# Cross-attention's query as three rounded products, in a decoder block on one core

## What is computed

```python
def _layernorm(x, axis=-1, eps=1e-05):
    ...
    return (x - m) / jnp.sqrt(v + eps)

def _L0_xattn_ref(k, v, q, Wk, Wv, bv, Wq, bq, Wo, bo):
    kp = jnp.einsum('bsd,ed->bse', k, Wk)
    vp = jnp.einsum('bsd,ed->bse', v, Wv) + bv
    qp = jnp.einsum('bsd,ed->bse', q, Wq) + bq
    scale = 1.0 / jnp.sqrt(jnp.float32(kp.shape[-1]))
    scores = jnp.einsum('bqd,bkd->bqk', qp, kp) * scale
    probs = jax.nn.softmax(scores, axis=-1)
    ctx = jnp.einsum('bqk,bkd->bqd', probs, vp)
    return jnp.einsum('bqd,ed->bqe', ctx, Wo) + bo
...
x = x + _L0_attn_ref(_layernorm(x, axis=-1), ...)
x = x + _L0_xattn_ref(ctx_1024, ctx_1024, _layernorm(x, axis=-1), ...)
x = x + _L0_ffn_ref(_layernorm(x, axis=-1), ...)
```

## Time and profile before

| | |
|---|---|
| median of 3 runs | 2769.6 us |
| profiled execution, its own time | 2767.93 us |
| span of the profiled execution | 2766.1 us |
| mean granted TensorE clock | 0.972 |
| TensorE matmul busy | 2549.4 us (92%), 19090 records |
| VectorE busy | 1976.6 us (71%), 3087 |
| ScalarE busy | 1442.4 us (52%), 4247 |
| GpSimd busy | 862.9 us (31%), 811 |
| query of cross-attention on TensorE | 1024 records, 201.3 us |
| `xnxT` copies on ScalarE | 64, 31.0 us |

### The profile page before, as it was taken

One profiled execution on the slowest core, in us unless ns is written; L12 is line 12 of the kernel. 1 busy time (PEld: TensorE's weight loads), 2 busy tenths in 40 slices (PEclk: granted clock), 3 DMA queues, 4 the chain that ended last, 5 costly groups with the idle time before them and its releaser, 6 DMA issues.

```text
span 2766.1 us, 55689 instructions
## 1 busy us (share of the span) xinstructions
PE 2549.4 (92%) x19090; PEld 2107.2 (76%) x19090; DVE 1976.6 (71%) x3087; ACT 1442.4 (52%) x4247; POOL 862.9 (31%) x811
## 2 busy tenths in 40 slices
PE   5999999999999999999999999999999999999840
PEld 3678878887888788878887888788878887888620
DVE  4445778877777787777777787777777877776552
ACT  2445555555555555555555555555555555555343
POOL 0001333323333333233333332333333323233344
PEclk9999999999999999999999999999999999999965
DMA  6233455554444555444445454444454554443799
GB/s 188 57 79 80 108 133 128 134 129 137 123 121 115 132 126 136 129 134 123 124 115 132 124 137 129 132 128 121 117 132 123 137 129 131 127 122 105 198 213 201
DMA packets 131545, 358.88 MB, mean 130 GB/s; under 512 B 21908, under 2 KB 26516, under 8 KB 123269
## 3 DMA queue, kind: packets, MB, share of 16 engines
q0 software_dynamic: 63520, 160.60, 25.0%
q1 hardware_dynamic: 63190, 192.16, 24.7%
q10 hardware_dynamic: 4784, 5.46, 0.6%
HBM read 316.38 MB, written 41.78 MB: 129 GB/s over the span
## 4 chain that ended last, share of the span: by engine, by line
PE 78%; DVE 8%; ACT 5%; issue 4%; DMA 2%; POOL 1%; ACTq 1%; DVEq 0%; POOLq 0%
PE psX L1150 41%; PE psA L1150 17%; PE psA L1159 6%; PE psF L1150 5%; PE psA L1216 4%; PE psA L1239 3%; PE psX L1159 2%; ACT L769 1%; DMA vg<-in_L_ffn_aux_values,idx 1%; DVE xmax L955 1%; PE psF L1159 1%; DVE top L1006 1%; ACT xT_hi L687 1%; DVE oT_lo L902 1%; DVE idx L1009 1%
## 5 line engine op out<-in xcount | busy, mean ns | idle before, releaser
L613 POOL DMA_INDIRECT vg<-in_L_ffn_aux_values,idx x512 | 542.8, 1060 | 1208.1 <-issue 1071.3
L708 ACT ACTIVATE pa<-psA,nmax 112x224 f32<-112x224 f32 x1024 | 443.6, 449 | 191.3 <-DVE nmax L924 184.5
L924 DVE TENSOR_REDUCE nmax<-psA 112x4 f32<-112x896 f32 x256 | 267.2, 1086 | 151.8 <-PE psA L1216 151.8
L1035 DVE SCALAR_TENSOR_TENSOR agg<-vg,wt,agg 112x512 f32<-112x512 f32 x406 | 361.6, 891 | 10.7
L1150 PE MATMUL psX<-big,gT 128*112 128x375 f32 x1024 | 333.4, 478 | 0.6 <-ACT gT L735 0.6
L1150 PE MATMUL psX<-pT,cx 125*128 125x224 f32 x1536 | 299.1, 355 | 0.0
L1150 PEld LDWEIGHTS psX<-pT,cx 125*128 125x128 f32 x1536 | 288.0, 190 | 4.0 <-issue 0.3
L939 DVE TENSOR_TENSOR pa<-pa,rsum 112x896 f32<-112x896 f32 x256 | 279.6, 1092 | 8.8
L1150 PEld LDWEIGHTS psX<-big,gT 128*112 128x112 f32 x1024 | 175.5, 176 | 125.7 <-issue 0.9
L1159 PE MATMUL psA<-ident,pa 112*112 112x112 f32 x2048 | 229.4, 263 | 24.9 <-DVE oT_lo L902 24.9
L1159 PEld LDWEIGHTS psA<-ident,pa 112*112 112x112 f32 x2048 | 202.0, 134 | 57.2 <-DVE oT_lo L902 31.5
(11 more groups left out here) (211 smaller groups left out, 5915.7 us busy)
## 6 DMA issues: line engine op xcount, KB each, us to landing
big<-in_ctx_t SPq DMA_DIRECT2D x32, 1500.0 KB, 6.3
cx<-in_ctx SPq DMA_DIRECT2D x32, 1344.0 KB
xa<-in_x SPq DMA_DIRECT2D x64, 224.0 KB, 2.9
centered<-in_x_t SPq DMA_DIRECT2D x32, 448.0 KB, 4.6
x<-in_L_attn_bff POOLq DMA_DIRECT2D x32, 448.0 KB
x<-cb_scratch POOLq DMA_DIRECT2D x32, 448.0 KB, 5.7
x<-in_x SPq DMA_DIRECT2D x31, 448.0 KB, 5.1
out<-x SPq DMA_DIRECT2D x30, 448.0 KB, 3.3
```

What stands on the lines that cost most here:

```text
L613: pool.indirect_dma_start(vg[:, c % SLOTS, k, :], None, aux_values, bass.IndirectOffsetOnAxis(ap=idx[:, t, n:n + 1], axis=0))\
L708: last = nc.scalar.activation(pa[:, t, h, :], psA[0:R, h, t * S:(t + 1) * S], ACT.Exp, bias=nmax[:, k % 2, h, t:t + 1], accum_out=rsum[:, ...
L924: nc.vector.tensor_reduce(nmax[:, k % 2, h:h + 2, :], psA[0:R, h:h + 2, 0:T * S].rearrange("p h (t s) -> p h t s", t=T), AX_X, ALU.max, ne ...
L1035: last = nc.vector.scalar_tensor_tensor(dst, vg[:, c % SLOTS, k, :], w, dst, ALU.mult, ALU.add)
```

## The change

The query becomes a `product3`. At set-up ScalarE rounds each chunk of the folded weight (with the scale) to `m1_hi` and VectorE makes `m1_lo` from the bank; before, VectorE alone wrote the chunk. In each batch ScalarE's two copies of the turned rows become rounding casts into `xnxT_hi`, which no longer free the bank but count `xn_hi`; VectorE gets a step in `("X", "turn")`, `x_turn_lo`: two subtractions that read the bank and `xnxT_hi`, write `xnxT_lo`, and free the bank. `xnxT_lo` lies over `oT_hi`, and `m1_hi` over the old `m1`. No table of order is changed. Cut to its core:

```diff
@@ -162,7 +162,9 @@
         wff_at = (nc.sbuf_base + 31) // 32 * 32
         wffT = (sb("wff_hi", [P, C, D], F32R), sb("wff_lo", [P, C, D], F32R))
         over_wff = nc.alloc_sbuf_tensor_at("over_wff", [P, 2 * C, D], F32, offset=wff_at)
+        m1_at = (nc.sbuf_base + 31) // 32 * 32
         m1 = sb("m1", [P, C * D])
+        m1T = (nc.alloc_sbuf_tensor_at("m1_hi", [P, C, D], F32R, offset=m1_at), sb("m1_lo", [P, C, D], F32R))
         m2_at = (nc.sbuf_base + 31) // 32 * 32
         m2 = (sb("m2_hi", [P, C, D], F32R), sb("m2_lo", [P, C, D], F32R))
         over_m2 = nc.alloc_sbuf_tensor_at("over_m2", [P, 2 * C, D], F32, offset=m2_at)
@@ -190,6 +192,7 @@
         rsum = sb("rsum", [R, NB, T, HB])
         pa = sb("pa", [R, T, HB, S])
         paT = sb("paT", [R, T, HB, S])
+        oT_at = (nc.sbuf_base + 31) // 32 * 32
         oT = (sb("oT_hi", [P, C, S], F32R), nc.alloc_sbuf_tensor_at("oT_lo", [P, C, S], F32R, offset=centered_at))
         big = sb("big", [P, C * SK])
         cxT = big[:, :].rearrange("p (c k) -> p c k", c=C)
@@ -200,7 +203,8 @@
         xnf = xnx
         px = nx[:, :].rearrange("p (t k) -> p t k", t=T)
         xnxT_at = (nc.sbuf_base + 31) // 32 * 32
-        xnxT = sb("xnxT", [P, C, S])
+        xnxT = (sb("xnxT_hi", [P, C, S], F32R), nc.alloc_sbuf_tensor_at("xnxT_lo", [P, C, S], F32R, offset=oT_at))
+        over_xnxT = nc.alloc_sbuf_tensor_at("over_xnxT", [P, C, S], F32, offset=xnxT_at)
         gT_at = (nc.sbuf_base + 31) // 32 * 32
         gT = sb("gT", [P, C, S])
         uT = (nc.alloc_sbuf_tensor_at("uT_hi", [P, C, S], F32R, offset=xnxT_at),
@@ -273,6 +277,7 @@
         summed, agg_stored = sem("summed"), sem("agg_stored")
         xT_hi, qk_hi, rq_hi, uT_hi, oT_hi = (sem(f"{n}_hi") for n in ("xT", "qk", "rq", "uT", "oT"))
         m2_hi, wff_hi, wff_split = sem("m2_hi"), sem("wff_hi"), sem("wff_split")
+        m1_hi, xn_hi = sem("m1_hi"), sem("xn_hi")
         small_loaded, mask_loaded = sem("small_loaded"), sem("mask_loaded")
         steps = {s: sem(f"dve_step_{s}") for s in "NAXFG"}
         log_done, lsum_spread, mean_full = sem("log_done"), sem("lsum_spread"), sem("mean_full")
@@ -384,8 +389,7 @@
         qw = cx[:, C * D:(C + 1) * D]
         rwT = gT[:, 0, 0:RS]
         over_d = gT[:, 1, 0:P]
-        bv_rows = xnxT[:, :, 0:R]
-        m1v = weight(m1)
+        bv_rows = over_xnxT[:, :, 0:R]
 
 
         CENTERED = 3
@@ -680,6 +684,12 @@
                         copy_out(s, job, b, dst[:, 2 * j:2 * j + 2, :], chunks(s, job))
                 return step
 
+            def x_turn_hi(b, _):
+                for j in range(2):
+                    job = FILL["X", "turn", 0] + j
+                    wait_full(act, "X", job, b)
+                    nc.scalar.copy(xnxT[0][:, 2 * j:2 * j + 2, :], chunks("X", job)).then_inc(xn_hi, 1)
+
             def center_hi(b, _):
 
                 act.wait_ge(xt_scaled, b + 1)
@@ -799,6 +809,10 @@
                 act.wait_ge(setup_full, ROUTED + c + 1)
                 nc.scalar.copy(m2[0][:, c, :], spare(ROUTED + c)).then_inc(m2_hi, 1)
 
+            def m1_hi_half(_, c):
+                act.wait_ge(setup_full, BIASED + c + 1)
+                nc.scalar.activation(m1T[0][:, c, :], spare(BIASED + c), ACT.Copy, scale=float(D) ** -0.5).then_inc(m1_hi, 1)
+
             def log_var(*_):
                 act.wait_ge(var_taken, B)
                 nc.scalar.activation(var_all[:, :], var_all[:, :], ACT.Ln, bias=1.0, accum_out=lsum[:, :])\
@@ -825,9 +839,9 @@
                 last.then_inc(scaled, 1)
 
             pipeline(act, {("Z", "log"): log_var, ("Z", "gate"): logits, ("Z", "scale"): scale,
-                           ("W", "split"): split_hi, ("W", "wff"): wff_hi_half, ("W", "m2"): m2_hi_half, ("N", "center"): center_hi, ("A", "mix"): mixed,
+                           ("W", "split"): split_hi, ("W", "wff"): wff_hi_half, ("W", "m2"): m2_hi_half, ("W", "m1"): m1_hi_half, ("N", "center"): center_hi, ("A", "mix"): mixed,
                            ("A", "qk"): qk, ("Q", "qk"): qk, ("A", "value"): value, ("A", "score"): exp_scores, ("A", "prob"): probs_turned,
-                           ("X", "turn"): turn("X", "turn", xnxT), ("X", "query"): query,
+                           ("X", "turn"): x_turn_hi, ("X", "query"): query,
                            ("X", "score"): x_exp, ("X", "prob"): x_probs_turned, ("X", "mix"): x_mixed,
                            ("F", "turn"): turn("F", "turn", xnfT), ("F", "route"): route, ("F", "score"): f_score,
                            ("F", "top"): f_top})
@@ -948,6 +962,13 @@
                 wait_full(dve, "X", j, b)
                 nc.vector.tensor_tensor(x1[:, t, :], bank("X", j)[0:R, :], x1[:, t, :], ALU.add)\
                     .then_inc(drained["X"][j % banks["X"]], 1)
+
+            def x_turn_lo(b, _):
+                for j in range(2):
+                    job = FILL["X", "turn", 0] + j
+                    dve.wait_ge(xn_hi, 2 * b + j + 1)
+                    lo(xnxT[1][:, 2 * j:2 * j + 2, :], bank("X", job)[:, 0:2 * S].rearrange("p (c s) -> p c s", c=2),
+                       xnxT[0][:, 2 * j:2 * j + 2, :]).then_inc(drained["X"][job % banks["X"]], 1)
 
             def x_maxima(b, t):
                 for j in range(2):
@@ -1089,7 +1110,9 @@
                 nc.vector.tensor_tensor(cb[:, :], made_next()[0:R, :], cb[:, :], ALU.add).then_inc(setup_drained, 1)
 
             def made_m1(_, c):
-                nc.vector.tensor_scalar(m1v[:, c, :], made_next(), float(D) ** -0.5, None, ALU.mult).then_inc(setup_drained, 1)
+                dve.wait_ge(m1_hi, c + 1)
+                nc.vector.scalar_tensor_tensor(m1T[1][:, c, :], made_next(), float(D) ** -0.5, m1T[0][:, c, :].bitcast(F32),
+                                               ALU.mult, ALU.subtract).then_inc(setup_drained, 1)
 
             def made_gb(*_):
                 nc.vector.tensor_scalar(gb[:, :], made_next()[:, 0:C], float(D) ** -0.5, None, ALU.mult)\
@@ -1136,7 +1159,7 @@
                            ("N", "stat"): x_moments, ("X", "stat"): x_stat, ("F", "stat"): f_stat, ("N", "center"): center_lo, ("A", "qk"): qk, ("Q", "qk"): qk,
                            ("A", "score"): maxima, ("A", "share"): share, ("A", "mix"): o_lo,
                            ("X", "enter"): x_enter,
-                           ("X", "norm"): x_norm, ("X", "score"): x_maxima, ("X", "prob"): x_probs_turned,
+                           ("X", "norm"): x_norm, ("X", "turn"): x_turn_lo, ("X", "score"): x_maxima, ("X", "prob"): x_probs_turned,
                            ("X", "mix"): u_lo, ("X", "out"): x_out,
                            ("F", "norm"): f_norm, ("F", "route"): route, ("F", "learn"): learn, ("F", "top"): f_top,
                            ("G", "sum"): g_sum, ("F", "sum"): g_sum})
@@ -1258,8 +1281,8 @@
                     wait_free(pe, "X", job, b)
                     for k in range(2):
                         i = 2 * j + k
-                        last = product(bank("X", job)[:, k * S:(k + 1) * S],
-                                       [(m1v[:, c, i * P:(i + 1) * P], xnxT[:, c, :]) for c in range(C)])
+                        last = product3(bank("X", job)[:, k * S:(k + 1) * S],
+                                        [(both(m1T, ALL, c, slice(i * P, (i + 1) * P)), both(xnxT, ALL, c, ALL)) for c in range(C)])
                     filled("X", job, last)
 
             def x_scores(b, t):
```

## The result

| | before | after |
|---|---|---|
| median of the runs | 2769.8 us (2767.4 to 2774.8, 11 runs) | 2775.7 us (2772.0 to 2780.7, 11 runs) |
| profiled execution | 2767.93 us | 2772.72 us |
| one iteration, mean of 28 | 79.11 us | 79.35 us |

The ratio is 1.0023, with a 95% interval of 1.0014 to 1.0032: slower, by little more than the 0.2% that can be told from nothing.

What follows compares the result with a forecast made beforehand. TensorE was taken to set the time nearly everywhere. 29 iterations x 0.31 = 9.0, two x -0.62 = -1.2 and set-up 1.0 gave +8.8 us: median 2778.4, rounded down to 2778; range 2750 to 2789, likeliest case 2775 to 2784.

Steps and rivals of the forecast that it cites:

- TensorE, the query: Query of each batch: 48 rounded matmuls at 0.111 us take 5.33 us for 6.16, 0.83 less; ends 0.62 earlier.
- VectorE, the new wait: Two subtractions between nx and stats_F: stats_F starts 2.73 us later, 1.57 of it waiting for transposes and copies.
- Nmax at 1418.19: Maxima of the scores, behind the sums: lag 2.73 exceeds the 2.07 of cover, so start moves 0.66 from 1417.53.
- X score 1 starts 0.31 later: Second half of the cross scores: waits 0.9 us for its bank, starts 0.31 us later; whole iteration 0.31 longer.
- The early iterations: Second and third iterations, lacking sums or router: the lag is covered there, -0.62 us each.
- Set-up: Before the loop: four ScalarE casts ahead of the drains of the folded weight, +1.0 us, bounds 0 and 2.5.
- "nothing" for the last batch: Last batch, after the loop: waits some 0.8 us for the subtractions and saves 0.83, so nothing.
- The cover holds: Rival, sums ahead of nmax: shifted from GpSimd's addition, VectorE regains up to 1.97 us; 2751 us; chance 0.24.
- The 2727 that the prediction worked out from four passes: Query by the skill's four passes for true fp32: gain 32 x (1.54 - 0.21) = 43 us, 2727.
- It cancels: Rival: release edges 0.15 shorter or lag 0.2 smaller; -0.2 to +0.16 us per iteration, 2764 to 2775; chance 0.23.
- The wait grows: Rival: no overlap of subtractions, held second cast or late gathers; iteration 0.5 to 0.9 longer, 2784 to 2796; chance 0.11.
- The clock: Rival: new waits drop TensorE to 1.2 GHz for a stretch; in every iteration 80 us, 2850; chance 0.02.

Runs made afterwards that it cites:

- Experiment 3: The kernel of experiment 2, with VectorE still waiting in X turn until ScalarE has made both casts, without subtracting: 2763.45 us, ratio 0.9974.
- experiment 2: The change without its two subtractions, all three products taking the rounded rows (the rest of the rows left out): 2748.67 us, ratio 0.9921.
- experiment 4: The complete change with the two subtractions moved behind both passes of the router's statistics and ahead of their merging: 2753.52 us, ratio 0.9939.
- experiment 6: TensorE starts the query after the first subtraction: added to the kernel of experiment 4, 2747.02 us; added to the change as it is, 2774.28 us.

## Why the prediction was right

**TensorE, the query: right, the gain a little large.** 48 matmuls between 1413.36 and some 0.11 behind 1418.70 are 5.45 us with the first step of 0.21; the forecast was 5.33 and 0.06 for the first load. The query begins 0.05 behind the second subtraction, which ends at 1413.31, and not 0.14. In the chain of the change it ended 0.55 earlier than before, where 0.62 was forecast. Without a wait the chain has 5.37, so that the form alone saves 0.70 and not the 0.83 of the pace. The long first step is not the wait's doing: rounded matmuls begin so without one too, as in the kernel before:

```profile
1464.89 0.37 PE L1150 MATMUL psA<-xT_hi,wqT_hi 128*128 128x224 f32 x1
1465.10 0.28 PE L1150 MATMUL psA<-xT_lo,wqT_hi 128*128 128x224 f32 x1
```

That a short pass has a fixed part fits the trace of before: passes of 256 columns step every 0.115 us (27 steps from 1402.47 to 1405.58), those of 224 columns every 0.111, some 4% less for 12.5% fewer columns. The shapes of the weights differ as well (112 and 128 columns), so the size of that part is not shown.

**VectorE, the new wait: right to 0.01.** Idle 1.56 for 1.57. Stats_F starts 3.64 us behind the start of nx, before 0.92: a lag of 2.72 for 2.73.

**Nmax at 1418.19: right.** It starts at 1421.14, which is 1418.20 in the frame of before, with no idle. The accumulator read ends at 1428.92, or 1425.98, the number forecast.

**X score 1 starts 0.31 later: right in kind, too large.** It starts at 1428.97, or 1426.03 in the frame of before, 0.16 later than there. The term that was mis-sized is what lies between that read and the matmul, 0.14 from the earlier trace rows and 0.06 for the weight load. The matmul starts 0.05 behind the read, and the sixteen last 5.30 for 5.21: together 0.14 for 0.20. So the iteration grew by 0.25 us, not 0.31. The forecast "0.8 to 0.9" of waiting before qk 3 and X score 1 came to 0.71: 0.16 later, with a query that ended 0.55 earlier. The profile prints only 0.24 of it as idle, ahead of qk 3, since neighbouring records overlap; in the same way the wait ahead of the query, forecast as 0.1 to 0.2, shows only as a start 1.59 us behind that of the transposes, where it was 1.53.

**The early iterations: right, a little large.** From the copies of the first batch to those of the second before took 76.55 us and after 76.00: -0.55 for -0.62, and -0.56 in the next.

**Set-up: +0.79 for +1.0** by the first copies (145.25 and 146.04). The number is weak: the kernels with the weight split have their first copies between 145.8 and 148.1, those without at 144.8 and 145.3. It wasn't tried alone.

**The sum.** +0.79 - 0.55 - 0.56 + 28 x 0.245 = +6.5 at the copies of the 31st batch (2516.14 and 2522.68); the 32nd and last has them at +6.7, and the profiled execution ends at +4.8. The 1.9 that are missing lie behind those copies, where the prediction had nothing. In the chains of before and of after:

```profile
2593.91 8.08 PE psX L1150 x32
...
2617.97 9.21 DMA vg<-in_L_ffn_aux_values,idx
```

```profile
2601.30 8.64 PE psX L1173 x48
...
2625.94 7.37 DMA vg<-in_L_ffn_aux_values,idx
```

The prediction's "nothing" for the last batch was short by 1.2 us: TensorE waited 1.28 us ahead of its query for 0.62 before, and the 48 matmuls took 0.56 longer than the 32, at a granted clock of 0.63 for 0.78. A gather that landed in 7.37 us for 9.21 took that back and 0.6 more, and another 1.3 were won in the last 25 us, behind the issue of the last output. One row of either kernel does not tell whether the change did any of the two. So that the profiled execution came out 4.0 below its forecast of +8.8 is about half the smaller iteration (29 x 0.065 = 1.9) and about half a tail that was not forecast, and that half is luck; the medians say +5.9.

**The rivals.** *The cover holds* was to decide at a lag of 2.42 us. Experiment 3, with 2.31, is 0.16 us per iteration faster than before, and from there to the change 0.41 us of lag made 0.40 of time: level at 2.47. The mechanism was real and the margin 0.25 us where 0.31 was forecast. It did not come about, since addition and sums moved together: the slow pair of sums takes 3.54 us where it took 3.51. The Trainium skill (Perfetto Trace Analysis, Identifying the Most-Contended Engine) says to optimise the engine of highest occupancy first, and to judge TensorE's headroom by its weight loads. By either count it is TensorE in both kernels (matmuls 92%, weight loads 76% and 75%, VectorE 71% and 73%). Its saving came out in experiment 2, to the full 0.71 us, and in the change not at all. The 2727 that the prediction worked out from four passes had no support: experiment 2, with everything hidden, is at 2749. *It cancels* held 2764 to 2775, and the median lies 0.7 above it: the release that was 0.06 shorter and the tail had brought it close. By the iterations it is out, at +0.25 us where it had at most 0.16. *The wait grows* did not happen: the two subtractions overlap as taken, 1.16 us together. *The clock* stayed at 1.00 in the loop.

## What to carry to other kernels

An instruction that waits is priced by what is queued behind it on its own engine, up to the next place where that engine was idle anyway: here 2.72 us of lag against 2.07 of cover. Before a saving on the busiest engine is believed, go to that place and subtract. And where a wait is needed, put in front of it work that is ready and that nobody needs soon: the two passes of statistics, moved by one entry of the order, made a change that lost 6 us into one that gains 18, and an earlier start of the query added some 5 more, which it could not do before that.

## What was not expected

- **Releases differ by place.** From the end of ScalarE's accumulator read to the matmul that it lets go: 0.05 us here, 0.14 in the earlier trace rows. From the end of VectorE's second subtraction to the query: 0.05, and not the 0.14 of the earlier trace rows. From the second cast to a VectorE instruction behind a bare wait: 0.26 in experiment 3, where the subtraction that reads the cast's output started 0.04 behind it. Each such edge counts 29 times: 0.2 us is 6 us.
- **The first of a group of rounded matmuls** takes 0.37 us for 0.27, and the next starts 0.21 behind it, not 0.11, with a wait ahead of it (1413.36 in the change) and without one (1464.89 before).
- **The clock ate a gain at the start of experiment 2.** From the first batch's copies to the second's it took 78.30 us (146.33 to 224.63), against 76.55 before and 76.00 in the change; later iterations took 78.40. TensorE waits 1.9 us ahead of the transposes near 169.5 in each of the three, and the granted clock then falls to 0.50, 1.2 GHz; in the change it is back at 1.00 by 174, in experiment 2 only by 182. The first row is experiment 2, the second the change (columns as in the row of one iteration above):

```profile
172.00:183.00 11.00, 10.38 (x72) 8.39 (x71) 3.62 (x6) 4.77 (x15) 0.00 (x0) 0.55 0.09 37
```

```profile
172.00:183.00 11.00, 10.05 (x87) 9.09 (x88) 4.79 (x8) 6.62 (x23) 0.00 (x0) 0.91 0.06 25
```

Why it stayed low for longer there is not shown.

The fastest version is experiment 4 with the early query of experiment 6, 2747.0 us: 0.8% under the kernel before, with every product of the change in it.
